# Layer-norm statistics of three chunks in four moved from VectorE to ScalarE, with a shorter routing and tail

## What is computed

```python
x = _layernorm(x + _L0_attn_ref(x, Wq, Wk, Wv, Wo, rms_w), axis=-1)
x = _layernorm(x + _L0_xattn_ref(ctx_1024, x, ...), axis=-1)
x = _layernorm(x + _L0_ffn_ref(x, router_weight, gate_up_proj, down_proj), axis=-1)
```

## Time and profile before

| | us |
|---|---|
| median of 3 runs | 1309.66 (1308.24 to 1310.13) |
| the profiled execution's own time | 1305.59 |
| span of the profiled execution | 1303.8 |
| DVE busy | 1124.0 |
| PE busy | 1126.6 |
| POOL busy | 954.8 |
| ACT busy | 844.8 |

### The profile page before, as it was taken

The page is one execution under the profiler, slowest core; times in us unless marked ns, Lnnn a source line. Parts: engine busy times, 40 slices in busy tenths (PEclk is TensorE's granted clock), DMA queues, the critical chain, the costliest instruction groups (busy, mean ns, idle before and its releaser), DMA issues. The chain is left out here.

```text
span 1303.8 us, 19359 instructions
## 1 busy us (share of the span) xinstructions
PE 1126.6 (86%) x6421; PEld 751.5 (58%) x6421; DVE 1124.0 (86%) x1578; ACT 844.8 (65%) x1516; POOL 954.8 (73%) x748
## 2 busy tenths in 40 slices
PE   6789998889988989898787569999999999999940
PEld 2343434434434533345333459989999999998940
DVE  4689999889999899998999649988988888898837
ACT  5765567635757447674443358878888878888833
POOL 0799668978899888899897135877777777777644
PEclk9788998799988979998796569999999999999985
DMA  8338324441255232533312248999999999999988
GB/s 313 75 81 271 81 70 100 134 100 34 67 130 146 49 86 51 146 81 98 85 33 87 93 146 248 312 302 305 314 305 303 308 304 303 308 309 300 271 150 314
DMA packets 95138, 235.03 MB, mean 180 GB/s; under 512 B 18608, under 2 KB 18864, under 8 KB 94400
## 3 DMA queue, kind: packets, MB, share of 16 engines
q1 hardware_dynamic: 64320, 162.44, 40.9%
q0 software_dynamic: 30720, 71.36, 22.8%
HBM read 147.33 MB, written 52.85 MB: 154 GB/s over the span
## 5 line engine op out<-in xcount | busy, mean ns | idle before, releaser
L1117 POOL TENSOR_TENSOR dbu<-rep,bc 128x1024 f32<-128x1024 f32 x128 | 302.0, 2364 | 62.5 <-DVE hst L1292 30.8
L1292 DVE TENSOR_TENSOR_SCAN hst<-hst,dbu 128x512 f32<-128x512 f32 x256 | 298.9, 1213 | 30.9 <-POOL dbu L1117 16.2
L1769 POOL DMA_INDIRECT sum_rows<-ye,tokens x128 | 205.4, 1605 | 97.8 <-ACT ye L1845 52.0
L416 PE MATMUL y_ps<-dbu,cs 128*32 128x512 f32 x512 | 156.6, 695 | 77.9 <-DVE dbu L1298 54.9
L856 ACT ACTIVATE hst<-rep,small_sb 128x512 f32<-128x512 f32 x256 | 166.1, 684 | 70.5 <-DVE dbu L1298 70.2
L1761 POOL DMA_INDIRECT xe<-x_rows,tokens x128 | 152.0, 1187 | 72.9 <-issue 37.8
L454 PE MATMUL ring<-first_raw,xT 128*128 128x512 f32 x384 | 179.6, 613 | 1.9 <-ACT made L878 1.9
L1298 DVE TENSOR_TENSOR dbu<-hst,bc 128x1024 f32<-128x1024 f32 x128 | 156.7, 1224 | 4.4
L1811 PE MATMUL low<-xh,w1h 128*128 128x256 f32 x512 | 150.6, 294 | 0.0
L1811 PE MATMUL low<-xl,w1h 128*128 128x256 f32 x512 | 145.3, 284 | 0.0
L1811 PE MATMUL low<-xh,w1l 128*128 128x256 f32 x512 | 145.3, 284 | 0.0
(11 more groups left out here) (207 smaller groups left out, 2674.8 us busy)
## 6 DMA issues: line engine op xcount, KB each, us to landing
first_raw<-in_gate_up SPq DMA_DIRECT2D x64, 768.0 KB
rep<-made SPq DMA_DIRECT2D x256, 128.0 KB
second_raw<-in_down SPq DMA_DIRECT2D x64, 256.0 KB
bc<-bc_rows SPq DMA_DIRECT2D x64, 128.0 KB, 3.2
second_raw<-in_down SPq DMA_DIRECT2D x64, 128.0 KB
rows<-sum_rows SPq DMA_DIRECT2D x16, 512.0 KB, 9.9
sum_rows<-x2T SPq DMA_DIRECT2D x1, 4608.0 KB, 16.8
xT<-in_x_turned SPq DMA_DIRECT2D x16, 256.0 KB
```

The costliest lines, as they stand in the source:

```text
L416: ins = pe.matmul(y_ps[rows, :], sel, dbu[:, n % WORK, g, :], start=(k == 0), stop=(k == QUADS - 1))
L1117: pool.tensor_tensor(dbu[:, n % WORK, :, :], rep[:, i % 2, :, 1, :], bc[:, k, 0, :].unsqueeze(1).broadcast_to([P, 2, T]), ALU.mult).then_i ...
L1292: dve.tensor_tensor_scan(h, h, dbu[:, n % WORK, i, :], 0.0, ALU.mult, ALU.add).then_inc(scanned, 1)
L1769: pool.indirect_dma_start(sum_dram[e % SUMS], bass.IndirectOffsetOnAxis(ap=tokens[:, e, j:j + 1], axis=0), ye[:, e % YE, j, :], None, comp ...
```

## The change

- **Statistics.** For c = 0, 1, 2, `add_attention` ends behind the addition. In slot 1 of the next chunk ACT makes two passes over the row instead (`first_spread`): a copy scaled by -1/D that sums to minus the mean, then a square with that as bias that sums the squared deviations. Both write their elements into the next chunk's still unused x1. For c = 3 DVE's statistics stay.
- **One slot later.** For these three chunks `norm_root` goes from slot 0 to slot 2 on POOL, `first_norm` and the gates of c = 2 (and the last c = 3) go behind `decays(n + 3)` on ACT, and POOL's gates go one slot later.
- **Routing.** The eight largest logits are taken directly, and shifted by the largest (`near`); `match_replace` runs on shifted logits before the exponential. The sum over all 64, its reciprocal and the product with it go. ACT takes a second exponential, of the eight.
- **Tail.** DVE does the last gate itself. PE turns three quarters of three row blocks ahead of it. The logits of the last batch go into four banks, and DVE shifts and masks each block as it comes. The last update of the counts goes.

```diff
 # PE
+            def turn_last(b):
+                early = range(RING)
+                pe.wait_ge(y3_ready, MI * (b + 1) - 1)
+                for j in early:
+                    ps = to_fill(pe, f"yT{b}_{j}")
+                    for m in range(MI - 1):
+                        pe.transpose(ps[:, m * P:(m + 1) * P], y3[:, m, j * P:(j + 1) * P], ident)
+                pe.wait_ge(y3_ready, MI * (b + 1))
+                m = MI - 1
+                for j in early:
+                    ps = ring[place[f"yT{b}_{j}"] % RING]
+                    pe.transpose(ps[:, m * P:(m + 1) * P], y3[:, m, j * P:(j + 1) * P], ident)\
+                        .then_inc(fill_sem(f"yT{b}_{j}"), 1)
+                turn_back(b, range(RING, NT))
+            def rate_last(b):
+                for j in range(NT):
+                    taken(pe, f"x2T{b}_{j}")
+                    for k in range(KD):
+                        ins = pe.matmul(hst[:, j, 0:EXPERTS], turned_of(b, j)[:, k * P:(k + 1) * P], rT[:, k, :],
+                                        start=(k == 0), stop=(k == KD - 1))
+                    ins.then_inc(rated, 1)
+                    if j + 2 < NT:
+                        turn_rows(b, j + 2)
-            turn_back(B - 1, range(NT))
+            turn_last(B - 1)
...
-            rate_experts(B - 1, range(NT))
+            rate_last(B - 1)
 # ACT
+            def first_spread(t):
+                b, c = divmod(t, NT)
+                taken(act, f"wo{t}")
+                done = (NT - 1) * b + c + 1
+                act.activation(x1[:, c + 1, :], x1[:, c, :], ACT.Copy, scale=-1.0 / D, accum_out=mv[:, c, 0:1])\
+                    .then_inc(mean_steps, 1)
+                act.wait_ge(mean_steps, done)
+                act.activation(x1[:, c + 1, :], x1[:, c, :], ACT.Square, bias=mv[:, c, 0:1], accum_out=mv[:, c, 1:2])\
+                    .then_inc(spread_ready, 1)
...
-                act.activation(lsm[:, :, :], lsm[:, :, :], ACT.Exp).then_inc(exped, 1)
+                act.activation(prob[:, :, :], lsm[:, :, :], ACT.Exp)
+                act.activation(top[:, :, :], near[:, :, :], ACT.Exp).then_inc(exped, 1)
...
                     decays(n + 1)
...
+                    if c:
+                        first_spread(t - 1)
...
-                    if t:
+                    if c == 0 and b:
                         first_norm(t - 1)
-                    if c == 0 and b:
                         gate_z(b - 1, 2)
                         gate_z(b - 1, 3)
+
+                    decays(n + 3)
...
+                    if c:
+                        first_norm(t - 1)
                     if c == 2:
                         gate_z(b, 0)
                         gate_z(b, 1)
                     if c == 3 and last:
                         gate_z(b, 2)
-
-                    decays(n + 3)
 # POOL
-                        if k == 0 and t:
+                        if k == (2 if c else 0) and t:
                             norm_root(t - 1)
...
-                        if k in (2, 3) and c == 2:
-                            gate(b, k - 2)
-                        if k == 2 and c == 3 and last:
+                        if k in (3, 4) and c == 2:
+                            gate(b, k - 3)
+                        if k == 3 and c == 3 and last:
                             gate(b, 2)
...
-            gate(B - 1, 3)
 # DVE
             def add_attention(t):
...
+                if c < NT - 1:
+                    return
...
             def shift_logits(b):
...
-                own.step(dve.tensor_reduce(small[:, 0, :], logits, AX.X, ALU.max))
+                for j in range(NT):
+                    own.step(dve.max(top[:, j, :], logits[:, j, :]))
                 own.settle()
-                dve.tensor_tensor(lsm[:, :, :], logits, each(small[:, 0, :]), ALU.subtract).then_inc(drain_sem(f"logits{b}"), 1)
+                own.step(dve.tensor_tensor(near[:, :, :], top[:, :, :], top[:, :, 0].unsqueeze(2).broadcast_to([P, NT, TOPK]),
+                                           ALU.subtract))
+                dve.tensor_tensor(lsm[:, :, :], logits, each(top[:, :, 0]), ALU.subtract).then_inc(drain_sem(f"logits{b}"), 1)
+            def shift_last(b):
+                own = Chain(dve, route_steps, ROUTE_STEPS * b + PLACE_STEPS - ROUTE_STEPS)
+                for j in range(NT):
+                    dve.wait_ge(rated, (NT - 1) * b + j + 1)
+                    own.step(dve.max(top[:, j, :], hst[:, j, 0:EXPERTS]))
+                    own.settle()
+                    own.step(dve.tensor_scalar(near[:, j, :], top[:, j, :], top[:, j, 0:1], None, ALU.subtract))
+                    dve.tensor_scalar(lsm[:, j, :], hst[:, j, 0:EXPERTS], top[:, j, 0:1], None, ALU.subtract).then_inc(shifted, 1)
+                    for i in ((), (0, 1), (2,), (3,))[j]:
+                        own.settle()
+                        dve.wait_ge(shifted, i + 1)
+                        own.step(dve.match_replace(out=mask[:, i, :], in_to_replace=near[:, i, :], in_values=lsm[:, i, :],
+                                                   imm_value=1.0))
             def choose(b, own):
+                if b < B - 1:
+                    own.settle()
+                    taken(dve, f"logits{b}")
+                    for j in range(NT):
+                        own.step(dve.match_replace(out=mask[:, j, :], in_to_replace=near[:, j, :], in_values=lsm[:, j, :],
+                                                   imm_value=1.0))
+                own.settle()
+                dve.tensor_scalar(chose[:, :, :], mask[:, :, :], 0.0, None, ALU.is_gt).then_inc(masked, 1)
                 dve.wait_ge(exped, b + 1)
-                own.step(dve.tensor_reduce(small[:, 1, :], lsm[:, :, :], AX.X, ALU.add))
+                own.step(dve.tensor_reduce(small[:, 0, :], top[:, :, :], AX.X, ALU.add))
                 own.settle()
-                own.step(dve.reciprocal(small[:, 2, :], small[:, 1, :]))
+                own.step(dve.reciprocal(small[:, 1, :], small[:, 0, :]))
                 own.settle()
-                own.step(dve.tensor_tensor(prob[:, :, :], lsm[:, :, :], each(small[:, 2, :]), ALU.mult))
...
+                own.step(dve.tensor_tensor(lsm[:, :, :], prob[:, :, :], each(small[:, 1, :]), ALU.mult))
 # DVE, tail
+            dve.wait_ge(y_taken, MI * B)
+            dve.wait_ge(sz_ready, MI * B)
+            dve.tensor_tensor(y3[:, MI - 1, :], y3[:, MI - 1, :], sz[:, MI - 1, :], ALU.mult).then_inc(y3_ready, 1)
...
-            chain["route"] = shift_logits(B - 1)
+            chain["route"] = shift_last(B - 1)
```

More of the change, by code:

```diff
@@ L83 @@
 NORM2_STEPS = NT
-ROUTE_STEPS = 25
-PLACE_STEPS = 27
+ROUTE_STEPS = 22
+PLACE_STEPS = 24
 HOT_AT = ((2, 1), (2, 4), (3, 0), (3, 3))
@@ L230, in mixers @@
         top = sb("top", [P, NT, TOPK])
-        small = sb("small", [P, 4, NT])
+        near = sb("near", [P, NT, TOPK])
+        small = sb("small", [P, 2, NT])
         idxf = sb("idxf", [P, 2, NT, TOPK])
@@ L309, in mixers @@
         stats_ready = sem("stats_ready")
+        mean_steps = sem("mean_steps")
+        spread_ready = sem("spread_ready")
         rstd_ready = sem("rstd_ready")
@@ L948, in exponents @@
             def exponents(b):
-                taken(act, f"logits{b}")
-                act.activation(lsm[:, :, :], lsm[:, :, :], ACT.Exp).then_inc(exped, 1)
+                if b < B - 1:
+                    taken(act, f"logits{b}")
+                else:
+                    act.wait_ge(shifted, NT)
+                act.activation(prob[:, :, :], lsm[:, :, :], ACT.Exp)
+                act.activation(top[:, :, :], near[:, :, :], ACT.Exp).then_inc(exped, 1)
             make_rates()
@@ L1008, in _ @@
                         gate_z(b, 2)
-                    decays(n + 3)
-                    for j in hots_due(n + 3, 2):
-                        number_lows(j, hot[:, j % 2, 1, :, :])
                     if front:
@@ L1142, in _, with root @@
             roots = Chain(pool, root_steps)
-            def root(dst, src, done=None):
-                roots.step(pool.tensor_scalar(dst, src, 1.0, EPS, ALU.mult, ALU.add))
+            def root(dst, src, done=None, scale=1.0):
+                roots.step(pool.tensor_scalar(dst, src, scale, EPS, ALU.mult, ALU.add))
                 roots.settle()
@@ L1158, in norm_root @@
             def norm_root(t):
-                c = slice(t % NT, t % NT + 1)
-                pool.wait_ge(stats_ready, t + 1)
-                root(rstd[:, c], mv[:, t % NT, 1:2])
-                pool.tensor_scalar(shift[:, c], mv[:, t % NT, 0:1], rstd[:, c], -1.0, ALU.mult, ALU.mult).then_inc(rstd_ready, 1)
+                b, j = divmod(t, NT)
+                c = slice(j, j + 1)
+                if j < NT - 1:
+                    pool.wait_ge(spread_ready, (NT - 1) * b + j + 1)
+                else:
+                    pool.wait_ge(stats_ready, b + 1)
+                own, sign = (1.0 / D, 1.0) if j < NT - 1 else (1.0, -1.0)
+                root(rstd[:, c], mv[:, j, 1:2], scale=own)
```

(27 more changed lines are left out.)

7 lines of the change are left out of this document (6 added, 1 removed).

## The result

Four runs of each: 1335.61 us after (1331.93 to 1343.55), 1309.26 before (1308.24 to 1310.13), ratio 1.0216 (95% interval 1.0192 to 1.0240). The change is slower by 2.2%, some 28 us. The prediction was 1299.5 us, faster. The profiled execution took 1336.23 us, its span is 1334.4.

The account below looks back on a forecast made before the run. DVE and PE were taken as equally busy, with only the end of `mixers` counting. Gains of 0.4, 4.2 (c = 1), 0 (c = 2), 2.5 less 1.5 (c = 3) and 4.8 (tail), 10.4 us, gave about 1299.5, range 1294 to 1304.

Parts of the forecast that it names:

- So the logits come 2.8 us later … 1.6 in the third batch and 0.3 in the second: Chunks c = 1: ACT's norm waits for POOL's later root, delaying logits 2.8 us in the last batch, 1.6 and 0.3 earlier.
- ACT behind POOL decides: Rival, chance 0.08: `first_norm` behind `decays(n + 3)` waits for POOL in 12 chunks, 26 us lost, time about 1319.
- Routing: Loop, three batches: operations removed, `near` added at 0.5 us (bounds 0.2 and 2.5); net gain about 1.1, 2.3 and 3.5.
- c = 1: nearly all, 0.8 each: Statistics taken off DVE in four chunks c = 1: nearly all saved, 0.8 us each, half counted in the first batch.
- c = 0 at nothing: Statistics taken off DVE in four chunks c = 0: no gain, since DVE waits for POOL's inputs for c = 1 anyway.
- Two passes, 1.6 for two, cost 0: Two summing passes on ACT behind `decays(n + 1)`: 1.6 us for both, covered before step 2's decays, so cost 0.
- 0 for the pair: Chunks c = 2: statistics gain nearly nothing, the convolution's tap comes 0.7 us behind DVE's need; together taken as 0.
- c = 3: Chunks c = 3: 1.5 us lost in the second batch, 2.5 gained in the last, 0 in the first and third.
- The sum: Whole kernel: the terms' gains and losses together save 10.4 us, from 1309.66 to about 1299.5.
- Tail, 4.8: Tail after the loop: 0.8, 3.3 and 0.7 us gained in three parts, 4.8 together, bounds 3 and 6.5.
- for a whole instruction: DVE beside POOL: a two-SBUF-input DVE operation and a POOL operation reading SBUF exclude each other for one whole instruction.

Follow-up runs that it names:

- tail_only: The kernel before with the change's new tail alone, the loop's routing, statistics and norm as before: 1305.15 us, ratio 0.9965.
- routing_tail: The changed kernel with statistics back on DVE and norm root, norm and gates in their old places, so only routing and tail are new: 1309.34 us, ratio 0.9993.
- near_last: routing_tail with two subtractions in the loop exchanged: first the one reading the logits' PSUM bank, then `near`; 1302.04 us, ratio 0.9948.
- no_stats: near_last with the first norm's statistics left out on any engine for three chunks of four: 1301.90 us, ratio 0.9960.

## Why the prediction was wrong, step by step

- **"So the logits come 2.8 us later … 1.6 in the third batch and 0.3 in the second"** is the step that failed. The first logits come 6.35 us later in the last batch, 5.31 in the third and 3.79 in the second, and these three chunks grow by 8.6, 8.0 and 6.4 us; putting the norm behind the copies gives back 20.0 of these 23. Up to the copy the working was right: it has the last batch's first copy done at 603.7, 17.9 us into its chunk, and it was done 17.8 us into it. What failed is the overlap behind it. I followed the copy only into `rate_experts` and took the 2.2 us that had lain between the two (598.7 and 600.86) as slack, 3.7 in the second batch. But `mix_values` needs the bank of the first copy, and it, the intra-chunk product (L508) and the logits stand in one row behind it on PE. So no part of the delay is absorbed, and PE's longer idle time adds 1.45 us by the lower clock in the last batch.
- **The rival "ACT behind POOL decides"** (0.08) was the course it took, with place and direction right and a price too low: 1319 against 1335.6. What I held against it, ACT's 41.3 us of waiting for mixed values, was no slack: that wait is itself the end of the chain that the norm delayed.
- **Routing.** The gain of 1.1 to 3.5 us per batch was a loss of some 3.7 in all (tail_only against routing_tail). The sizes are also not quite those of its own terms, which give 1.1, 2.4 and 3.7. `near` at 0.5 with the bound 2.5 measured 1.14 to 3.52, and 1.14 in all three places of the change. But its length was not the error, since near_last keeps the stall and is faster than the kernel before: the step that failed is where it stands, ahead of the operation that frees a bank. That step was not in the working at all. In the right order the loop's routing gives perhaps 2 us (0.9948 against 0.9965 for the tail alone; the intervals overlap).
- **"c = 1: nearly all, 0.8 each"** for the statistics: 0, by no_stats. "DVE has no wait from the logits to the end of the chunk" was read from idle time; DVE does wait there, inside `prev` and `idxf`, where a wait for POOL looks like work. c = 0 at nothing was right.
- **"Two passes, 1.6 for two, cost 0"**: 0.61 + 0.19 and 0.72 + 0.19, overlapped about 1.5 us; right. Their cost is at most what POOL's root waits for them.
- **c = 2, "0 for the pair"**: wrong in the third batch by 4.0 us; the other three grew by 1.0, 0.8 and 0.7. **c = 3**: +1.5 in the second batch measured +0.1, and -2.5 in the last -1.4.
- **The sum** gives 1299.3 and not 1299.5; nothing hangs on it.
- **Tail, 4.8**: 4.70 in the change's profile, by its parts. By tail_only 4.6 in time, but 3.6 in its own profile, as in most others (33.5 us): right in place, and in size within what the runs can tell. Timeline of the changed kernel, against the earlier trace rows:

```profile
752.12 2.18 PE L544 MATMUL ring<-cs,y 128*128 128x128 f32 x9
754.09 0.85 PE L549 MATMUL ring<-cs,y 128*128 128x128 f32 x3
...
754.62 0.69 DVE L1432 TENSOR_TENSOR x<-ring,x 128x512 f32<-128x512 f32 x1 [0.91 <-PE ring L549]
...
767.79 0.22 DVE L1460 MAX8 top<-hst 128x8 f32<-128x64 f32 x1
...
769.25 0.40 PE L591 MATMUL ring<-chose,below 128*128 128x256 f16 x1 [1.53 <-DVE chose L1479]
```

From `take_y` (752.23, before 721.91) to the first sum 2.39 for 3.37: 0.98 gained (0.8). From the last logits to PE's counting 1.46 for 4.48: 3.0 gained (3.3). From there to the end 15.36 for 16.07: 0.7 (0.7).

So the version that beats both kernels takes the routing and tail without the moves, and the bank freed first: near_last, 0.9948.

## What to carry to other kernels

When a step is moved behind another engine's queue, follow what stands behind it through the ring of PSUM banks, not through the data alone: here a copy that only the router seemed to need also freed the bank of the next matmuls. Free a bank before any operation that can stall, however small that operation is. Work taken off the engine that looks full pays only if its next wait, also one hidden inside an instruction's length, does not take it back.

## What the runs showed of the hardware

- An operation of DVE with 32 elements stood 3.19 us beside POOL's products, past the end of one (610.97) and through the next, which followed without a gap; it ended when the second did (612.19). `prev` was held in the same way by an indirect DMA and the product 0.02 us behind it. In these rows the wait lasts until POOL leaves a gap of 0.17 us, and a gap of 0.02 did not end it. The prediction's "for a whole instruction" is too short.
- Of DVE's small operations beside a POOL product, those with two SBUF inputs (`near`, `prev`) and a `tensor_scalar` from SBUF to SBUF (3.5 us for eight elements) waited; MAX8 with one SBUF input and the subtraction from PSUM did not (0.61 for four, 0.42).
- After 3.7 us in which PE did nothing the granted clock of the next 11.2 us was 0.71 on the mean, 0.50 at first and 1.00 at the end, and 16 matmuls took 9.50 us instead of 7.11. After 6.57 us without work two groups of matmuls took 3.52 us that took 2.07 before.
